# A cross-attention and feed-forward layer on one core: the prologue rewritten with plain fp32 gates, x read in place, and maxima spread by TensorE

## The reference

```
q = layernorm(x);  k = v = ctx
pre = 15 tanh((concat(q, k, v) @ ifgate_w.T + ifgate_b) / 15)      # 8 input gates i, 8 forget gates f
lf  = cumsum(log_sigmoid(f))
log_d[t, s] = lf[t] - lf[s] + i[s]   where t >= s, else -inf
m = max over s of log_d;  d = exp(log_d - m)
s_mat = (q @ k.T / sqrt(32)) * d
h = s_mat @ v / (max(|sum(s_mat)|, exp(-m)) + 5e-5)
x = x + h / rms(h) * (1 + outnorm_w)                               # rms per head
y = layernorm(x)
y = silu(w1 y) * (w2 y);  y = gelu(h1 y);  y = gelu(h2 y)          # 256 -> 1024 -> 1024 -> 1024
x = x + w3 y                                                       # 1024 -> 256
```

## Time and profile before

| | |
|---|---|
| time, median of 3 runs | 851.47 us (849.77 to 852.13) |
| the profiled execution, its own time | 851.26 us |
| its span, first to last instruction | 849.5 us |
| PE busy | 805.2 us (95%) |
| VectorE busy | 564.8 us (66%) |
| ScalarE busy | 380.3 us (45%) |
| GpSimd busy | 61.0 us (7%) |
| mean granted clock of TensorE | 0.96 of full speed |

### The profile page before, as it was taken

How to read it: one execution, slowest core, us unless ns; L and a number is a source line. 1 busy time by engine, 2 the same in 40 slices (tenths; PEclk the granted TensorE clock), 3 DMA queues, 4 the chain that set the end, 5 groups by cost and what they waited for, 6 DMA issues and landing times.

```text
span 849.5 us, 11813 instructions
## 1 busy us (share of the span) xinstructions
PE 805.2 (95%) x4610; PEld 689.1 (81%) x4610; DVE 564.8 (66%) x1336; ACT 380.3 (45%) x551; POOL 61.0 (7%) x54
## 2 busy tenths in 40 slices
PE   6276999999999999999999999999999999999996
PEld 5276888888888888887888888887888888887886
DVE  4957485957857585957857585857857583865553
ACT  2320462356535463355545463455535463335331
POOL 4320000100020000200020000200020000000000
PEclk7756899999999999999999999999999999999999
DMA  8485000121000400122000400122000400250540
GB/s 270 193 347 197 2 26 2 50 119 56 26 27 32 167 26 1 51 101 75 26 26 26 174 3 24 51 101 75 25 27 25 151 1 1 104 169 26 154 145 26
DMA packets 14634, 66.39 MB, mean 78 GB/s; under 512 B 2032, under 2 KB 2416, under 8 KB 11504
## 3 DMA queue, kind: packets, MB, share of 16 engines
q1 hardware_dynamic: 13280, 54.07, 18.0%
q0 software_dynamic: 1296, 11.53, 3.4%
HBM read 57.08 MB, written 8.52 MB: 77 GB/s over the span
## 4 chain that ended last, share of the span: by engine, by line
PE 80%; DVE 16%; ACT 2%; issue 2%; DMA 0%; POOL 0%; DVEq 0%; ACTq 0%
PE ps_f L1140 22%; PE ps_f L1141 21%; DVE decay L741 8%; PE ps_a L1079 7%; PE ps_f L1116 7%; PE ps_f L1117 7%; PE ps_f L1173 4%; PE ps_f L1174 4%; DVE decay L757 2%; PE ps_a L1061 2%; PE ps_a L998 2%; PE ps_a L1070 1%; PE ps_a L1089 1%; PE ps_a L1035 1%; PE ps_a L1028 1%
## 5 line engine op out<-in xcount | busy, mean ns | idle before, releaser
L1140 PE MATMUL ps_f<-h_hi,wgt 128*128 128x512 f32 x1024 | 404.0, 395 | 0.0
L1141 PE MATMUL ps_f<-h_lo,wgt 128*128 128x512 f32 x1024 | 399.1, 390 | 0.0
L1140 PEld LDWEIGHTS ps_f<-h_hi,wgt 128*128 128x128 f32 x1024 | 192.4, 188 | 40.2
L1141 PEld LDWEIGHTS ps_f<-h_lo,wgt 128*128 128x128 f32 x1024 | 192.4, 188 | 38.0
L850 DVE TENSOR_TENSOR h_lo<-work,h_hi 128x512 fp32r<-128x512 f32 x128 | 86.5, 690 | 135.0 <-ACT h_hi L569 133.9
L564 ACT ACTIVATE work<-ps_f,scl 128x512 f32<-128x512 f32 x128 | 87.5, 683 | 161.3 <-PE ps_f L1141 161.1
L1116 PE MATMUL ps_f<-h_hi,wgt 128*128 128x512 f32 x256 | 101.6, 397 | 0.0
L1117 PE MATMUL ps_f<-h_lo,wgt 128*128 128x512 f32 x256 | 100.4, 392 | 0.0
L551 ACT ACTIVATE work<-ps_f,scl 128x512 f32<-128x512 f32 x64 | 44.1, 688 | 93.3 <-PE ps_f L1117 93.3
L569 ACT ACTIVATE h_hi<-work 128x512 fp32r<-128x512 f32 x128 | 80.9, 632 | 4.1
L841 DVE SCALAR_TENSOR_TENSOR work<-ps_f,scl,work 128x512 f32<-128x512 f32 x64 | 48.1, 751 | 49.9 <-ACT work L551 49.9
(11 more groups left out here) (148 smaller groups left out, 759.1 us busy)
## 6 DMA issues: line engine op xcount, KB each, us to landing
decay<-m_rows SPq DMA_DIRECT2D x16, 1024.0 KB, 6.0
decay<-w_cols SPq DMA_DIRECT2D x22, 512.0 KB, 4.2
wgt<-w_cols POOLq DMA_DIRECT2D x5, 1024.0 KB, 9.6
v_aug<-ctx_tok SPq DMA_DIRECT2D x8, 528.0 KB, 3.6
z<-x SPq DMA_DIRECT2D x8, 512.0 KB, 4.4
xs<-x SPq DMA_DIRECT2D x8, 512.0 KB, 3.6
wgt<-w_cols POOLq DMA_DIRECT2D x2, 2048.0 KB, 12.8
x_kept<-xs SPq DMA_DIRECT2D x8, 512.0 KB, 2.6
```

Source lines behind the costliest of these rows:

```text
L1140: pe.matmul(ps_f[:, bank], w, moving(h_hi[layer][:, k], as_is), start=(k == 0), stop=False)
L1141: last = pe.matmul(ps_f[:, bank], w, moving(h_lo[layer][:, k], as_is), start=False, stop=(k == KH - 1))
```

## The change

The prologue is written anew; the loop of batches keeps its work and order.

- **x.** The first two pairs' x go straight into the tiles `xs`, where the residual needs them later, and the norms read them there and write `z`. Before, x was loaded into `z` as well.
- **Gates of pairs 0 and 1.** Plain fp32 products, four for the keys and four for z, with the gate weights placed by GpSimd in a small zeroed tile (`gw_plain`). No splitting of keys, z or gate weights ahead of them; `split_gate_weights` runs later, for pair 2.
- **Maxima of pair 0.** PE multiplies a broadcast column of the identity with the 16 rows of maxima, one product of 256 columns for each of 16 heads and sequences, into `ps_f`; `masks(0)` reads PSUM. No roundtrip through memory for pair 0.
- **Banks.** The second sequence's scores of pair 0 go to `ps_f`, and the four values blocks of pair 0 have a bank each. `make_state(0)` waits only for the first sequence's weighed scores.
- **Order.** VectorE norms pair 1 before the scans of pair 0; floors, the gain and the split of gate weights move behind the state and the scans of pair 1. GpSimd issues its first six weight loads in one go, behind `place_gate_weights`.

```diff
+        gw_in = num[:, 512:512 + 3 * CH * 2 * HEADS].rearrange("p (c g) -> p c g", g=2 * HEADS)
+        gw = num[:, 608:608 + 2 * CH * 2 * HEADS].rearrange("p (c g) -> p c g", g=2 * HEADS)
+        gw_plain = num[:, 672:672 + 2 * CH * 2 * ROW_FLOOR].rearrange("p (c g) -> p c g", g=2 * ROW_FLOOR)
...
+        def gate_out(j):
+
+            return ps_a[:, 3 if early(j) else 2, 0:SEQ]
+
+        def rows_out(j):
+
+            return (ps_f[:, 0] if early(j) else ps_a[:, 2])[:, SEQ:SEQ + TILES * ROWS]
+
+        def spread_out(h):
+            return ps_f[:, h // 2, h % 2 * SEQ:(h % 2 + 1) * SEQ]
+
+        def score_out(j, b, rowgrp):
+
+            return ps_f[:, rowgrp] if first(j) and b else ps_a[:, rowgrp]
+
+        def value_out(j, b, t):
+
+            if first(j):
+                return (ps_f if b else ps_a)[:, 2 + t, 0:HEADS * DV]
+            return ps_a[:, 2 + b, 0:HEADS * DV]
...
-            load_z(0)
+            load_x(0)
...
-            load_z(1)
+            load_x(1)
             load_ctxT(1)
             load_v(0)
...
-            keep_rows(0)
-            spread_max(0)
...
+            def place_gate_weights():
+
+                pool.wait_ge(s_gw, 16)
+                pool.wait_ge(s_gw_plain, 1)
+                dst = gw_plain.rearrange("p c (k e) -> p c k e", k=2)[:, :, :, HEADS:2 * HEADS]
+                src = gw_in.rearrange("p c (k g) -> p c k g", k=2)
+                pool.tensor_copy(dst[:, 0:CH], src[:, 0:CH]).then_inc(s_gw_plain, 1)
+                pool.tensor_tensor(dst[:, CH:2 * CH], src[:, CH:2 * CH], src[:, 2 * CH:3 * CH], ALU.add).then_inc(s_gw_plain, 1)
+
...
-            load_weights((0, 1))
...
-            split_keys_low(0)
-            split_normed_low(0)
-            load_weights((2, 3))
-            split_keys_low(1)
-            split_normed_low(1)
-            load_weights((4, 5))
+            place_gate_weights()
+            load_weights((0, 1, 2, 3, 4, 5))
...
-                act.wait_ge(s_gate_sum, j + 1)
-                act.activation(rows[0:GATE_COLS], gate_sum(j), ACT.Tanh, bias=gb[:], scale=1.0 / CAP).then_inc(s_gact, 1)
+                if plain(j):
+                    act.wait_ge(s_gate, j + 1)
+                else:
+                    act.wait_ge(s_gate_sum, j - W + 1)
+                act.activation(rows[0:GATE_COLS], gate_out(j)[0:GATE_COLS] if plain(j) else gate_sum, ACT.Tanh, bias=gb[:], scale=1.0 / CAP).then_inc(s_gact, 1)
...
-            split_keys(0)
             take_zT(0)
             act.wait_ge(s_gb, 1)
-            take_gate_low(0)
             soft_cap(0)
             softplus(0)
+            act.preload_act_table_set("exp_and_others")
+            take_zT(1)
             take_cols(0)
             decay_cols(0)
-            split_keys(1)
-            take_zT(1)
-            decays(0)
-            take_gate_low(1)
+            decays(0, 0)
             soft_cap(1)
+            decays(0, 1)
             softplus(1)
...
+                        if first(j):
+                            dve.wait_ge(s_spread, CH * b + c + 1)
                         for h in range(c * ROWGRP, (c + 1) * ROWGRP):
                             for t in range(TILES):
                                 part = decay_of(b, h, t)
                                 row = ROW_G + b * HEADS + h
-                                last = dve.scalar_tensor_tensor(part, part, cols[:, t, row:row + 1], future[:],
+                                maxima = spread_out(h)[:, t * P:(t + 1) * P] if first(j) else part
+                                last = dve.scalar_tensor_tensor(part, maxima, cols[:, t, row:row + 1], future[:],
...
-            split_gate_weights()
             dve.wait_ge(s_const, 16)
             dve.tensor_scalar(gb[:], gb_in[:], 1.0 / CAP, None, ALU.mult).then_inc(s_gb, 1)
-            add_gate_low(0)
-            scan_f(0)
-            scan_m(0)
             norm_1_stats(1)
             norm_rsqrt(s_norm1, 1)
             norm_1_apply(1)
-            dve.wait_ge(s_gain, 16)
-            dve.tensor_scalar(gain_b[:], gain_b[:], 1.0, None, ALU.add).then_inc(s_gain, 1)
+            scan_f(0)
+            scan_m(0)
             dve.wait_ge(s_ident, 8)
             masks(0)
-            floors(0)
             weigh_scores(0, 0)
-            add_gate_low(1)
             weigh_scores(0, 1)
             take_state(0)
             scan_f(1)
             scan_m(1)
+            split_gate_weights()
+            floors(0)
+            dve.wait_ge(s_gain, 16)
+            dve.tensor_scalar(gain_b[:], gain_b[:], 1.0, None, ALU.add).then_inc(s_gain, 1)
...
+            def plain_gates(j, source, base):
+
+                to = gate_out(j)[0:GATE_COLS]
+                for b in range(W):
+                    at = slice(HEADS * (1 - b), HEADS * (1 - b) + GATE_COLS)
+                    for c in range(CH):
+                        last = pe.matmul(to, gw_plain[:, base + c, at], source[:, c, b * SEQ:(b + 1) * SEQ],
+                                         start=(base == CH and b == 0 and c == 0), stop=(base == 0 and b == W - 1 and c == CH - 1))
+                return last
+
+            def plain_gates_keys(j):
+                pe.wait_ge(s_gw_plain, 3)
+                pe.wait_ge(s_ctxT[j], 16)
+                plain_gates(j, ctxT(j), CH)
+
+            def plain_gates_normed(j):
+                pe.wait_ge(s_zTe, j + 1)
+                plain_gates(j, zT(j), 0).then_inc(s_gate, 1)
+
+            def spread_maxima(b, heads_of):
+
+                for h in heads_of:
+                    row = b * HEADS + h
+                    last = pe.matmul(spread_out(h), ident[0:BH, row:row + 1].to_broadcast([BH, P]), m_row(0),
+                                     start=True, stop=True)
+                return last
...
+                    if first(j):
+                        pe.wait_ge(s_gact, GATE_STEPS + 1)
+                elif first(j):
+                    pe.wait_ge(s_mask, MASK_STEPS)
...
-                pe.wait_ge(s_smat, SMAT_STEPS * j + SMAT_STEPS)
+                pe.wait_ge(s_smat, SMAT_STEPS * j + (ROWGRP if first(j) else SMAT_STEPS))
...
-            keep_clock(12)
+            keep_clock(20)
+            plain_gates_keys(0)
+            plain_gates_keys(1)
             turn_z(0)
-            gates(0)
-            keep_clock(12)
+            plain_gates_normed(0)
+            keep_clock(8)
+            turn_z(1)
+            keep_clock(8)
+            pe.wait_ge(s_scan, 3)
+            pe.wait_ge(s_zTe, 2)
+            spread_maxima(0, range(0, 2))
             pe.wait_ge(s_cleared, 1)
             turn_rows(0)
-            turn_z(1)
+            spread_maxima(0, range(2, 4)).then_inc(s_spread, 1)
+            spread_maxima(0, range(4, 8)).then_inc(s_spread, 1)
+            pe.wait_ge(s_mask, 1)
+            spread_maxima(1, range(0, 4)).then_inc(s_spread, 1)
+            plain_gates_normed(1)
+            pe.wait_ge(s_mask, 2)
+            spread_maxima(1, range(4, 8)).then_inc(s_spread, 1)
             scores(0, 0)
-            gates(1)
             scores(0, 1)
             make_state(0)
-            for b in range(W):
-                values(0, 0, b)
+            values(0, 0, 0)
+            values(0, 1, 0)
             read_state(0)
-            for b in range(W):
-                values(0, 1, b)
+            values(0, 0, 1)
+            values(0, 1, 1)
             turn_rows(1)
-            keep_clock(24)
+            keep_clock(24, 1)
             turn_z2(0)
-            keep_clock(8)
+            keep_clock(8, 1)
```

More of the change, by code:

```diff
@@ L294, in load_z @@
             def load_z(j):
-                reuse(sp, s_zT, j)
+                sp.wait_ge(s_zT, j)
+                if j == 2:
+                    sp.wait_ge(s_mst, 16)
                 sp.dma_start(z[:], x[j]).then_inc(s_zin, 16)
@@ L307, in load_x @@
             def load_x(j):
-                if early(j):
-                    sp.wait_ge(s_scan, SCAN_STEPS * 2)
-                    sp.wait_ge(s_mst, 16 * 2)
                 reuse(sp, s_out, 16 * (j - 1))
@@ L531, in decay_cols, with decays @@
                 last.then_inc(s_ecols, 1)
-            def decays(j):
-                for n in range(EXP_STEPS):
+            def decays(j, b):
+                for n in range(CH * b, CH * (b + 1)):
                     act.wait_ge(s_mask, MASK_STEPS * j + n + 1)
@@ L672, in norm_1_stats @@
             def norm_1_stats(j):
-                dve.wait_ge(s_zin, 16 * j + 16)
-                norm_stats(s_norm1, j, z)
+                if plain(j):
+                    dve.wait_ge(s_xin[j], 16)
+                else:
+                    dve.wait_ge(s_zin, 16 * (j - W) + 16)
+                norm_stats(s_norm1, j, xs[j] if plain(j) else z)
             def norm_1_apply(j):
-                norm_apply(j, z, z, s_z)
+                if early(j):
+                    dve.wait_ge(s_zT, j)
+                norm_apply(j, xs[j] if plain(j) else z, z, s_z)
             def norm_2_stats(j, src):
@@ L734, in masks @@
                 for b in range(W):
```

(21 more changed lines are left out.)

78 lines of the change are left out of this document (40 added, 38 removed).

## The result

The changed kernel takes 841.47 us (median of 4 runs, 840.74 to 841.95), the kernel before, on the same chip, 851.80 (4 runs, 849.77 to 852.19). The ratio is 0.9882, 95% interval 0.9867 to 0.9897: 10.3 us faster, where 17.8 were forecast. The profiled execution took 841.54 with a span of 839.7, 9.8 shorter than before.

What follows compares the result with a forecast made beforehand. The bound was the 90.6 us prologue, where engines wait in turn before the first feed-forward product. Starting it 18.2 earlier, less 0.6 clock loss, gains 17.6: 851.26 - 17.6 = 833.7 us; range 827 to 841, forecast case 830 to 837.

Steps and rivals of the forecast that it cites:

- D: Milestone: first feed-forward product, end of the prologue; forecast at 72.4 us against 90.59, 18.2 earlier.
- A: Milestone: first gates ready, when pair 0's x half of the gate product ends; forecast at 16.0 us against 18.6.
- B: Milestone: mask of pair 0 done; forecast at 32.4 us against 41.56, a gain of 9.2.
- C: Milestone: numerators of pair 0 complete, after the values products; forecast at 51.1 us against 69.30.
- loss behind D: Feed-forward start: the full clock may come up to 3 us late, losing 0.5 per us; 0.6 us taken.
- four spreads 1.7 at full clock, so VectorE leads: Mask of pair 0: four spreads take 1.7 us, eight mask instructions 2.12, so VectorE sets the pace.
- pair 1's gate half: PE during pair 0's mask: pair 1's gate products, priced at 1.7 us, come before the fourth spread.
- the full clock for the first nine pieces: Values products of pair 0: full clock lasts for nine pieces, then half; 1.0 us saved.
- the second: Rival: PE cold or late early, turn and gate products slower; 5 us, 839 (836 to 842), chance 0.24.
- The first rival: Full clock holds through the values products, VectorE's queue then ends the stage, 6.4 earlier; 827, chance 0.16.
- The third: Rival: no change, something unseen such as weight loads sets the first feed-forward product; 851, chance 0.04.
- The fourth: Rival: slower, the feed-forward starts at half clock and stays there; 50 us of it give 858, chance 0.04.

Runs made afterwards that it cites:

- 128-row spreads: Changed kernel with its 16 spread products contracting over all 128 rows, the added rows zeroed, instead of 16 rows; 833.79 us, ratio 0.9798.
- 16-row and the 33-column fillers: Changed kernel with the 24 fillers behind the values cut to 16 rows, or to 33 moving columns; one run each, 841.86 and 843.46 us.
- the run at 829.10: Profiled run of the kernel with 128-row spreads and the z half of pair 1's gate product moved behind the last spreads; median 831.43 us.
- the first roundtrip kernel: Changed kernel with pair 0's maxima sent through memory again instead of spread by PE, weight loads left ahead; 852.51 us, ratio 1.0008.

## Why the prediction was right or wrong

The sign, the gain's place and the part behind D were right. The size was not: 7.8 us too much. Milestone by milestone:

| | predicted us | measured | us too early in the forecast, by stage |
|---|---|---|---|
| A | 16.0 | 17.26 | 1.3 |
| mask starts | 23.0 | 25.08 | 0.8 |
| B | 32.4 | 39.32 | 4.8 |
| C | 51.1 | 60.09 | 2.1 |
| D | 72.4 | 80.94 | -0.4 |
| loss behind D | 0.6 | 0 | -0.6 |

**The failed step** is "four spreads 1.7 at full clock, so VectorE leads", and with it the 1.7 for "pair 1's gate half". The clock fell at 25.00. The second and third groups of spreads ran at half clock, 3.4 for four, and the gate half took 3.65. PE led instead: waits of 0.73, 1.25 and 3.41 us stand in VectorE's brackets, 5.4 us, where the step had one of 0.85. The price of a product was right (427 ns at full, 853 at half, whatever its rows: the estimate for the broadcast tile held), and the row of the mask too (270 ns from PSUM against 265). The 128-row spreads show the cause: one edit, clock held, 7.7 us back.

A warning lay in front of me. The earlier trace rows show PE busy 15.50 of 15.50 us at half clock, with 33-column products, and I wrote that being busy alone did not raise the clock. I then used that for the values and not for the spreads, which use an eighth of the array's rows. The Trainium skill, "TensorE: Matmul & The Clock Gate", What's actually happening, has the chip set the clock by how busy PE has been. The 16-row and the 33-column fillers, 8.00 of 8.00 us busy at 0.50, disagree with that if busy means the profile's busy time, as far as fp32 products go. What was missing is not how busy, but with what.

**B to C**, 2.1: "the full clock for the first nine pieces" (1.0) did not come true: the clock had fallen again at 38.66, 5.1 us ahead of the first value product, and make_state, 2.10 at half rate where the forecast had 1.1, was on the path. **A**, 1.3: the clock's first rise, which I took from before at 5.9, came at 7.94, so the fillers ended at 9.5 and not 8.3, and the keys of pair 1 at 13.1 and not 12.2. (The terms of A in the forecast add up to 15.8; 0.2 of its 16.0 has no term.) Pair 1's keys were not late in landing; PE had no wait for them. The loss of up to 0.6 behind D did not occur: the clock was up at 79.62, 1.3 us ahead of D.

**What was right:** the second norm is hidden in VectorE's wait (10.22 to 15.82, scan at 20.11), the mask starts 8.0 earlier, the floors and the split weights lie behind the weighing and cost nothing (the last of them ends at 49.16, 10.9 us ahead of C), C to D is nearly unchanged (20.85 against 21.29), and the chain through PE and VectorE ahead of D sets the time.

**The norm of pair 1.** The forecast puts the gain of moving it at 7.8 us (not to be confused with the miss of the same size), and that gain was not the norm's alone. The issue of the two broadcasts in the timeline of the kernel before, and the times to landing from the view of their tile:

```profile
27.02 0.80 SPq L327 DMA_DIRECT2D decay<-m_rows  x2
```

```profile
DMA to landing us min/median/max: 4.2/5.3/6.5
```

So with the norm gone and the roundtrip kept, the mask could have started near 31.2, only 1.9 us sooner. The forecast names the roundtrip but gives it no price of its own.

**The rivals.** In its number the second came closest (839), but not in its mechanism: the turn and the first gate products ran at full clock (1.09 and 1.93), and the fall came 12 us later, in the spreads. Of its rule on transposes no run says anything. The first rival, warm values, did not occur in the changed kernel; two edits on, with PE's clock held by the spreads, it did, in the run at 829.10. The third, no change, with something unseen such as the weight loads setting D, did not occur: D came 9.65 us earlier. The weight loads do have that power, though: with the loads moved forward as this change moves them and the roundtrip kept, the time is 852.51, no change. The fourth, a feed-forward that stays at half clock, did not occur either.

So the change is three that hang together. The plain gates and the early norm bring the mask's inputs forward: with them, the roundtrip kept and the loads out of its way, the kernel takes 837.45 us against 850.17 before (they were not tried one by one). The bunched weight loads would have taken it all back over the roundtrip. The spreads over PE cut that knot, and gave much of it away through the clock. The best version here has 128-row spreads and pair 1's gate product behind them: 831.4 us, 20 less than before and 10 less than the changed kernel.

Open: why the clock lasts through the values in some runs and falls in others, by the mean clocks even of the same kernel. In the five profiles with 128-row spreads it falls at 36.04 (ahead of make_state), 39.21, 39.74 and 42.13 (amid the values) and only at 54.47, behind them; all five have PE idle for 1.3 to 1.8 us ahead of make_state. That its first rise wanders too (5.1 to 8.0 us, under fillers that start at 2.07 to 2.12) suggests a phase that the kernel does not set; that was not tested.

## What to carry to other kernels

Where a short stage waits for PE, look at what each product holds and not only at how long it takes: one over 16 rows costs the time of one over 128, and zero rows that change no sum can keep the clock for what follows. Do not price a stage at a clock that only the stage ahead of it shows. Judge a transfer that PE work is to replace beside the loads in flight: replacing it by the 16-row spreads was worth 11 us with the weight loads ahead of it, and cost 4 against the kernel with them behind it. (The 128-row spreads, at 833.79, are still 3.7 ahead of that kernel.)

## What the runs showed of the hardware that was not expected

- At the same busy share the clock rose under some fp32 products and not under others. 48 pieces of 128 rows and 128 moving columns: up after 3.2 us, 7.11 in all. With 16 rows 10.61, with 33 moving columns 10.37, no rise. But 33-column pieces can run at full rate once the clock is up (32 in 3.65).
- GpSimd's weighing of the keys, two instructions, takes 1.19 us with VectorE idle (at 23.18 in the first roundtrip kernel), 1.18 with most of it beside a mask read from PSUM (at 24.68 in the changed kernel) and 4.72 beside the same mask read from SBUF (32.07 above); the mask itself loses little, 8.70 against 8.47 for 32. The Trainium skill, "SBUF — State Buffer", Who interferes with whom, says that a VectorE instruction with two SBUF inputs contends with a GpSimd one that reads SBUF; the traces agree. In the earlier trace rows it is VectorE that suffers, 2.30 us for an instruction of 0.17 that has only one input, so that row is not this rule's.
- Two broadcast loads of 1 MB each landed 12.6 and 18.5 us after the first was issued beside the weight loads (398 GB/s), and 4.3 and at most 7.2 us after it with those held back (the mask's start at 27.04, and GpSimd, which waited for both, at 29.92). The 16 KB store ahead of them took 5.0 and 1.4 us.
